# Layer 1: the output's affine step and its gate moved behind the transpose, with channels on partitions

## The chip, the cores and the metric

The kernel runs on one NeuronCore of one Trainium2 chip. The metric is the device time of one execution in microseconds (us); the time of the kernel before is the median of three executions.

## The reference, cut to what matters

Two transformer-like layers are applied to x, [8, 256, 256] (8 sequences of 256 tokens, 256 channels). The change lies in the attention half of layer 1, in its last lines:

```python
xc = silu(conv(xn) + conv_b)                       # causal conv of 4 taps, per channel
i_gate = sigmoid(xc @ ig_w.T + ig_b)
gamma  = sigmoid(xc @ gamma_w.T + gamma_b)
mem[t] = gamma[t] * mem[t-1] + i_gate[t] * k[t] * v[t]   # scan over tokens
out = _ln(mem, mn_g, mn_b) * q
o = (out - mean) / sqrt(var + 1e-05)               # per head of 16 channels
o = o * gn_g + gn_b                                # per channel (256)
o = o * sigmoid(xc @ og_w.T + og_b)                # output gate
return o @ Wo.T
```

The feed-forward half of layer 1 (704 hidden units, ternary weights) runs beside it on the same normalised input.

## The kernel before

Layer 0 comes first and fills the first two thirds of the program; the change does not touch it. A short preparation block then loads and splits the weights of layer 1 (a float32 matrix is carried as a high and a low part, `..._hi` and `..._lo`, and a product is three products of parts). Layer 1 follows in one block. The 2048 tokens are cut in GROUPS = 4 groups of 512 tokens (GT), each two sequences (`b` = 0, 1) or four tiles of 128 tokens (`t` = 0 to 3).

The groups are run as a software pipeline. `turns` calls `turn(late, early)` with (None, 0), then three times in a hardware loop with (i, i + 1), then with (3, None). The early part of a turn does projections, convolution, norms, gates and the feed-forward of a group; the late part does the scan, the two norms behind it, the output product and the store of the group before. So there are five turns: the first with an early part alone, three loop turns with both, and the last with a late part alone. In this text they are turn 0, loop turns 1, 2 and 3, and the last turn.

Each engine has its own instruction stream, written out by hand in one order per turn, and works it in that order. Between engines there are only semaphores: `wait(name, k)` holds the engine until `name` has been raised k times in this turn; `inc` raises it. A held instruction holds all behind it on its engine.

PSUM has eight banks, `lbank` in the profile. The four tiles' gate products take banks 2 and 3 in turn (`gate(t)`): 128 tokens on partitions, 256 columns of input gate and 256 of output gate, with both biases added by one more matmul (`ones_rows` by `bias`, L1673). The scalar engine's sigmoid (L1333) writes both halves to `gates`. `gated(engine, late, b)` (L1196 to L1203) is the affine step and the gate, three tensor-by-tensor operations on [128, 512] in SBUF, recorded in the profile at L1151; the gain and the shift lie in `par`, copied to all partitions. GpSimd does it for b = 0 and the vector engine for b = 1. `o_turn(b)` (L1697) then transposes `o` by TensorE into bank 4 + b, `output_high` (scalar engine, L1348) and `output_low` (vector engine, L1528) split it, and `output(b)` multiplies by Wo (L1591), `residual(b)` (L1536) adds x, and SyncE stores.

Names that the prediction uses, on each engine in program order, at the end of a loop turn: on the vector engine `output_normed` (its last operation is L1523), `hidden(4)` (L1469), `gated(1)`, `hidden(5)`, `values(1)` (four operations at L1151: two on `rows` with `par`, two on `qk`), `output_low(0)` and `(1)`, `residual`, `mlp_added`. On TensorE `gate(0)`, `gate(1)`, `ffn_up(5)` (L1641, which waits for `hidden(4)`), `gamma(1)`, `o_turn(0)`, `o_turn(1)`, `gate(2)`, `gate(3)`, `output(0)`, `output(1)`, `ffn_down` (L1655). On the scalar engine `sigmoid(5)` (L1290), `gate(0)`, `gate(1)`, `output_high(0)`, `hidden_high(5)` (L1297), `output_high(1)`, `decays(1)` (L1314), `gate(2)`, `gate(3)`. On GpSimd `gated(0)`, `hidden_low(4)`, `hidden_low(5)` (L1167), `through_input_gate(0)` and `(1)` (L1184).

Of the kernel before, what the change touches and what calls it, by code (L numbers as in the profile page):

```python
# [15 lines left out]
P = 128  # L16
D = 256
# [41 lines left out]
G16, G256 = 4 * L1_DH, 2 * D  # L59
N_LOADS = 6  # L60
# [871 lines left out]
def layer1(nc, dram, keep, out):  # L932

    X, ident = keep["X"], keep["ident"]
    with ExitStack() as ctx:
        def sb(name, shape, dt=F32):
# [12 lines left out]
        bias = sb("bias", [P, 2 * D], F32R)  # L949
        conv = sb("conv", [P, KC, TAPS + 1])  # L950
        gamma_b = sb("gamma_b", [P, KC])
        par = sb("par", [P, G16 + G256])
        vn_g, vn_b, mn_g, mn_b = (par[:, L1_DH * n:L1_DH * n + L1_DH].rearrange("p (a d) -> p a d", a=1)
                                  .to_broadcast([P, PAIR_HEADS, L1_DH]) for n in range(4))
        gn_g, gn_b = par[:, G16:G16 + D], par[:, G16 + D:G16 + 2 * D]
        gn_g2, gn_b2 = (x.rearrange("p (a d) -> p a d", a=1).to_broadcast([P, BPG, D]) for x in (gn_g, gn_b))
# [16 lines left out]
                   vn_done=BPG, gamma_done=KC, decay_done=KC, io_done=TPG, gates_done=TPG,  # L973
# [5 lines left out]
                   ro_done=1, on_done=BPG, o_link0=2, o_link1=2, o_done0=1, o_done1=1,  # L979
# [3 lines left out]
        with ExitStack() as prep:  # L983
# [7 lines left out]
            bias_raw = tmp("bias_raw", [P, 2 * D])  # L991
            bias_b = tmp("bias_b", [P, 2 * D], F32R)
# [4 lines left out]
            @block.sync  # L997
            def _(sp):
                sp.dma_start(shared[:], dram["l1w"].rearrange("p k n -> p (k n)")).then_inc(once["raw_loaded"], 16)
                sp.dma_start(rows3[:].bitcast(BF16)[:, 0:3 * UPC], dram["signs"]).then_inc(once["signs_loaded"], 16)  # L1000
                sp.wait_ge(once["zeroed"], 1)
                loads = [(const2[:], dram["const2"]), (wo_raw[:], dram["wo"]),
                         (conv[:], dram["conv"]), (gamma_b[:], dram["gamma_b"])]
                loads.append((par[:], dram["scales_shifts"].partition_broadcast(P)))
                loads.append((bias_raw[0:2, :], dram["gate_bias"]))
                assert len(loads) == N_LOADS
                for dst, src in loads:
                    sp.dma_start(dst, src).then_inc(once["loaded"], 16)
                prime(sp, list(S.values()))

            @block.gpsimd
            def _(pool):
                pool.memset(bias_raw[:], 0.0).then_inc(once["zeroed"], 1)
                pool.memset(half[:], -0.5).then_inc(once["zeroed"], 1)
                pool.memset(eps16[:, 0:2 * PAIR_HEADS], 0.0).then_inc(once["zeroed"], 1)
# [11 lines left out]
                pool.tensor_scalar(gn_g, gn_g, 4.0, None, ALU.mult)  # L1027
                pool.wait_ge(once["w_hi_done"], 2)
                pool.tensor_tensor(wo_lo[:], wo_raw[:], wo_hi[:].bitcast(F32), ALU.subtract).then_inc(once["w_lo_done"], 1)
# [49 lines left out]
        gates = sb("gates", [P, 2, TPG, D])  # L1079
# [100 lines left out]
        def through_input_gate(engine, early, b):  # L1180
            wait = waiter(engine, early)
            wait("gates_done", 2 * b + 2)
            wait(f"kv_done{b}", 1)
            inc(engine.tensor_tensor(vn[:, pair(b), :], qk[:, 1, pair(b), :], gates[:, 0, pair(b), :], ALU.mult), f"b_done{b}")  # L1184
# [30 lines left out]
        @block.gpsimd  # L1215
        def _(pool):
            pool.memset(xpad[:, :, :, 0:PAD], 0.0).then_inc(pad_zeroed, 1)

            def turn(late, early):
                def convolved():  # L1220
                    wait = waiter(pool, early)
                    for k in range(KC):
                        wait("conv_sig", k + 1)
                        inc(pool.tensor_tensor(cs[:, k, :], cv[:, k, :], cs[:, k, :], ALU.mult), "xc_done")
                    for k in range(KC):
                        wait("xc_hi_done", k + 1)
# [12 lines left out]
                if late is not None:  # L1239
                    gated(pool, late, 0)  # L1240
                if early is not None:
                    hidden_low(pool, early, 4)
                    hidden_low(pool, early, 5)
                    through_input_gate(pool, early, 0)
                    through_input_gate(pool, early, 1)

            turns(pool, turn)

        @block.scalar
        def _(act):  # L1250
            act.wait_ge(pad_zeroed, 1)

            def turn(late, early):
# [45 lines left out]
                def convolved():  # L1299
# [4 lines left out]
                    wait("io_done", 0)  # L1304
# [20 lines left out]
                def gate(t):  # L1325
                    wait = waiter(act, early)
                    wait("io_done", t + 1)
                    if t == 0:
                        wait("o_done0", 0)
                        wait("o_done1", 0)  # L1330
                        wait("b_done0", 0)
                        wait("b_done1", 0)
                    inc(act.activation(gates[:, :, t, :], turned(banks[2 + t % 2][:]), ACT.Sigmoid), "gates_done")  # L1333
# [39 lines left out]
                if early is not None:  # L1373
# [5 lines left out]
                    gate(0)  # L1379
                    gate(1)  # L1380
                if late is not None:
                    output_high(0)
                if early is not None:
                    hidden_high(5)
                if late is not None:
                    output_high(1)
                if early is not None:
                    decays(1)
                    gate(2)
                    gate(3)  # L1390
# [4 lines left out]
        def _(dve):  # L1395
            def turn(late, early):
# [171 lines left out]
                if late is not None:  # L1568
                    gated(dve, late, 1)
                if early is not None:  # L1570
                    hidden(5)
                    values(dve, early, 1)
# [12 lines left out]
        def _(pe):  # L1585
# [15 lines left out]
            def turn(late, early):  # L1601
# [9 lines left out]
                def query_key(t):  # L1611
# [5 lines left out]
                    else:  # L1617
                        wait("gates_done", 0)
# [45 lines left out]
                def gate(t):  # L1664
                    wait = waiter(pe, early)
                    if t < 2:
                        wait("qk_sq", TPG)
                        wait("xc_lo_done", KC)
                    else:
                        wait("gates_done", t - 1)  # L1670
                    bank = banks[2 + t % 2][:]
                    product(bank, rows(xc_hi, xc_lo, t), cols(W_IO, W_G), last=False)
                    inc(pe.matmul(bank, ones_rows[:], bias[:], start=False, stop=True), "io_done")  # L1673
# [43 lines left out]
                if early is not None:  # L1717
# [12 lines left out]
                    gate(0)  # L1730
                    gate(1)
# [5 lines left out]
                if early is not None:  # L1737
                    gate(2)
                    gate(3)
# [24 lines left out]
def layouts(inputs, np):  # L1764
# [44 lines left out]
    a["scales_shifts"] = np.concatenate([l1["attn_" + n] for n in ("vn_g", "vn_b", "mn_g", "mn_b", "gn_g", "gn_b")]).reshape(1, -1)  # L1809
    a["gate_bias"] = np.repeat(np.concatenate([l1["attn_ig_b"], l1["attn_og_b"]]).reshape(1, -1), 2, axis=0)  # L1810
# [30 lines left out]
```

## Time and profile before

| what | value |
|---|---|
| median of 3 executions | 938.91 us (937.0 to 942.07) |
| profiled execution, its own time | 938.2 us |
| its span, first to last instruction | 936.4 us |
| mean granted clock of TensorE | 0.917 of full |
| busy: PE (TensorE) | 763.0 us |
| busy: DVE (vector engine) | 699.5 us |
| busy: ACT (scalar engine) | 452.4 us |
| busy: POOL (GpSimd) | 419.0 us |

Busy time is a sum over the whole program. Layer 1 begins with its preparation at about 611 us and its five turns run from about 629 us to the end; what one of its turns costs is read from the order of the work in that turn, not from these sums. The 1.8 us between span and time lie around the instructions.

### The profile page before, as it was taken

How to read it: one execution, taken by the hardware profiler on the slowest of the kernel's cores; microseconds unless marked ns; L12 is line 12 of the kernel's file. 1: busy time of each engine (PE TensorE's matmuls, PEld its weight loads, DVE VectorE, ACT ScalarE, POOL GpSimd, SP SyncE). 2: the span in 40 equal slices, each digit the busy share in tenths (PEclk: the TensorE clock that was granted, in tenths of full speed). 3: DMA queues.
4: the chain of work that ended last, by engine and by line, in shares of the span. 5: the costliest groups of instructions: out<-in, count | busy, mean ns of one | idle time of the engine just before them, and what ended most of it. 6: DMA issues, size and time to landing. Idle time of an engine off the chain costs nothing. (4 is left out here: it accounts for less than half of the span.)

```text
span 936.4 us, 15623 instructions
## 1 busy us (share of the span) xinstructions
PE 763.0 (81%) x5602; PEld 653.7 (70%) x5602; DVE 699.5 (75%) x1146; ACT 452.4 (48%) x717; POOL 419.0 (45%) x335
## 2 busy tenths in 40 slices
PE   3278989999999999999999999918683883893842
PEld 3166878888888888888888888806572672682642
DVE  6988866876776766776776766346689889879866
ACT  4256546556657556557556565535342342332301
POOL 2244533443466756662542543342616616606622
PEclk9999989999999999999999999958796896796775
DMA  4111210110110110110000000030000000000000
GB/s 150 34 35 36 86 42 25 53 42 2 30 36 19 47 42 19 47 30 3 20 18 12 11 19 3 1 147 1 1 1 0 8 15 0 0 22 0 0 22 23
DMA packets 21383, 25.82 MB, mean 28 GB/s; under 512 B 4418, under 2 KB 17090, under 8 KB 21060
## 3 DMA queue, kind: packets, MB, share of 16 engines
q1 hardware_dynamic: 21316, 24.93, 9.0%
q8 instruction: 41, 0.67, 0.3%
q14 instruction: 26, 0.21, 0.1%
HBM read 14.83 MB, written 3.28 MB: 19 GB/s over the span
## 5 line engine op out<-in xcount | busy, mean ns | idle before, releaser
L593 DVE TENSOR_REDUCE neg_max<-s_pair 128x4 f32<-128x1024 f32 x127 | 155.0, 1220 | 81.4 <-PE s_pair L805 81.1
L446 ACT ACTIVATE probs<-t_pair 128x1024 f32<-128x1024 f32 x128 | 131.3, 1026 | 139.8 <-PE t_pair L830 139.6
L345 POOL TENSOR_TENSOR hid<-g,hid 128x512 f32<-128x512 f32 x64 | 82.3, 1286 | 185.5 <-DVE g L704 143.9
L339 POOL TENSOR_TENSOR hid_lo<-hid,hid_hi 128x512 fp32r<-128x512 f32 x64 | 85.9, 1342 | 96.1 <-ACT hid_hi L456 96.0
L805 PE MATMUL s_pair<-K,Q 96*128 96x256 f32 x508 | 85.5, 292 | 14.0 <-DVE neg_max L593 9.4
L805 PEld LDWEIGHTS s_pair<-K,Q 96*128 96x128 f32 x508 | 76.6, 196 | 22.8 <-issue 7.3
L830 PE MATMUL t_pair<-Q,K 104*128 104x512 f32 x256 | 86.5, 420 | 0.3 <-DMA Q<-max_parts 0.3
L872 PE MATMUL down<-w_hi,hid_hi 128*128 128x256 f32 x256 | 83.9, 328 | 0.7 <-POOL hid_lo L339 0.7
L872 PE MATMUL down<-w_lo,hid_hi 128*128 128x256 f32 x256 | 72.1, 282 | 0.0
L872 PE MATMUL down<-w_hi,hid_lo 128*128 128x256 f32 x256 | 72.1, 282 | 0.0
L1151 POOL TENSOR_TENSOR rows<-rows,par 128x512 f32<-128x512 f32 x24 | 36.2, 1509 | 79.5 <-DVE rows L1499 52.4
L845 PE MATMUL misc<-probs,V 128*32 128x256 f32 x1024 | 69.1, 388 | 0.8 <-DVE xn_lo L543 0.5
L872 PEld LDWEIGHTS down<-w_hi,hid_hi 128*128 128x128 f32 x256 | 48.2, 188 | 26.4 <-issue 24.7
L1641 PE MATMUL lbank<-l_xn_hi,tern 128*128 128x512 f32 x96 | 38.0, 484 | 25.1 <-DVE l_hid L1469 25.1
L733 PE MATMUL gate<-xn_hi,w_hi 128*128 128x256 f32 x256 | 56.9, 304 | 0.0
L696 DVE SCALAR_TENSOR_TENSOR g<-g,gate 128x512 f32<-128x512 f32 x64 | 42.7, 668 | 18.6 <-ACT g L459 18.5
L467 ACT ACTIVATE g<-g 128x512 f32<-128x512 f32 x64 | 40.2, 628 | 26.6 <-DVE g L696 26.6
L733 PE MATMUL up<-xn_hi,w_hi 128*128 128x256 f32 x256 | 52.8, 289 | 0.0
L733 PE MATMUL up<-xn_lo,w_hi 128*128 128x256 f32 x256 | 52.3, 286 | 0.0
L733 PE MATMUL up<-xn_hi,w_lo 128*128 128x256 f32 x256 | 52.3, 287 | 0.0
L733 PE MATMUL gate<-xn_hi,w_lo 128*128 128x256 f32 x256 | 51.4, 282 | 0.0
L733 PE MATMUL gate<-xn_lo,w_hi 128*128 128x256 f32 x256 | 51.3, 282 | 0.0
(244 smaller groups left out, 2058.2 us busy)
## 6 DMA issues: line engine op xcount, KB each, us to landing
stage<-in_ternary SPq DMA_DIRECT2D x18, 256.0 KB, 2.9
Q<-q_hi SPq DMA_DIRECT2D x64, 64.0 KB, 2.0
stage<-in_scales SPq DMA_DIRECT2D x8, 384.0 KB, 3.4
X<-in_x SPq DMA_DIRECT2D x8, 256.0 KB, 3.7
Q<-q_lo SPq DMA_DIRECT2D x32, 64.0 KB, 2.0
Q<-max_parts SPq DMA_DIRECT2D x128, 4.0 KB
out<-res SPq DMA_DIRECT2D x8, 256.0 KB, 2.2
shared<-in_l1w SPq DMA_DIRECT2D x1, 1536.0 KB, 6.2
```

The lines of the kernel that those rows point to most:

```text
L339: pool.tensor_tensor(hid_lo[:, m % 2, :, :].rearrange("p a n -> p (a n)"), hid[:, m % 2, :], hid_hi[:, m % 2, :, :].rearrange("p a n -> p ...
L345: pool.tensor_tensor(hid[:, m % 2, :], g[:, m % 2, :], hid[:, m % 2, :], ALU.mult).then_inc(S["hid_done"], 1)
L446: act.activation(probs[:, u % 2, th, :], t_pair[:], ACT.Exp, scale=SCALE).then_inc(S["probs_done"], 1)
L467: act.activation(g[:, m % 2, :], g[:, m % 2, :], ACT.Tanh, scale=GELU_B).then_inc(S["t_done"], 1)
L593: dve.tensor_reduce(neg_max[:, u % 2, 4 * jp:4 * jp + 4], score_banks(u, jp)[:].rearrange("p (s n) -> p s n", n=SEQ), AX_X, ALU.max, negat ...
L696: dve.scalar_tensor_tensor(out=g[:, m % 2, :], in0=g[:, m % 2, :], scalar=1.0, in1=gate[:], op0=ALU.add, op1=ALU.mult).then_inc(S["u_done" ...
L733: mm = pe.matmul(out, lhs[a][k], rhs[b][k], start=(n == 0), stop=(n == 3 * KC - 1))
L805: mm = pe.matmul(score_banks(u, jp)[:, 512 * j + SEQ * s:512 * j + SEQ * s + SEQ], Q[0:KROWS, quad, 2 * jp + j, P * s:P * s + P], K[0:KROW ...
L830: mm = pe.matmul(t_pair[:, 512 * jp:512 * jp + 512].rearrange("p (j n) -> p j n", j=2), K[rows, quad, hq, P * th:P * th + P], Q[rows, quad ...
L845: mm = pe.matmul(misc[32 * j:32 * j + 32, 0:SEQ], V[:, th, h, :], probs[:, u % 2, th, SEQ * j:SEQ * j + SEQ], start=(th == 0), stop=(th == ...
L872: mm = pe.matmul(down[:, D * t:D * t + D], h[:, m % 2, n, P * t:P * t + P], w[:, a, n, 2 * D:3 * D], start=(a == 0 and t == 0 and n == 0 a ...
L1641: mm = pe.matmul(banks[bank][:], w[:, k, P * c:P * c + P], x[:, k, :], start=(n == 0), stop=(n == 3))
```

## The change

The affine step and the gate are done after the transpose, where a channel is a partition. The gain, the shift and the output gate's bias then are one number per partition (`out_cols`, a new small load). The steps are now:

- `o_turn(b)` waits for the normed output alone.
- `output_affine(b)`, scalar engine, new: two operations on [128, 256] from PSUM, with scale and bias from `out_cols`, to `oa` in SBUF.
- `output_gated(b)`, vector engine, new: one product of `oa` and `out_gate` on [128, 512], for both b. GpSimd has no part in it any more.
- `output_high` and `output_low` read `oa` instead of the PSUM bank.
- The gate products: `input_gate(b)` makes the input gate of two tiles in one bank (28 matmuls of 256 columns for all four, with the bias matmul as before); `output_gate(m)` makes the output gate of 128 channels by 512 tokens (6 matmuls of 512 columns each), with its bias in the scalar engine's sigmoid.

```diff
-        def gated(engine, late, b):
-            wait = waiter(engine, late)
-            wait("on_done", b + 1)
-            y = o[:, pair(b), :]
-            inc(linked(engine, wait, f"o_link{b}", [
-                (y, y, gn_g2, ALU.mult),
-                (y, y, gn_b2, ALU.add),
-                (y, y, gates[:, 1, pair(b), :], ALU.mult)]), f"o_done{b}")
...
-                if late is not None:
-                    gated(pool, late, 0)
...
+                def output_gate(m):
+                    wait = waiter(act, early)
+                    wait("og_done", m + 1)
+                    if m == 0:
+                        wait("o_done", 0)
+                    inc(act.activation(out_gate[:, m, :], banks[2 + m][:], ACT.Sigmoid, bias=out_cols[:, m, 2:3]), "out_gate")
...
+                def output_affine(b):
+                    wait = waiter(act, late)
+                    wait("o_turned", b + 1)
+                    for m in range(KC):
+                        inc(act.activation(oa[:, b, m, :], banks[4 + b][:, SEQ * m:SEQ * m + SEQ], ACT.Identity,
+                                           scale=out_cols[:, m, 0:1], bias=out_cols[:, m, 1:2]), "oa_done")
+
                 def output_high(b):
                     wait = waiter(act, late)
-                    wait("o_turned", b + 1)
-                    inc(act.activation(o_hi[:, b, :, :], turned(banks[4 + b][:]), ACT.Copy), "o_hi_done")
+                    wait("o_done", b + 1)
+                    inc(act.activation(o_hi[:, b, :, :], oa[:, b, :, :], ACT.Copy), "o_hi_done")
...
+                def output_gated(b):
+                    wait = waiter(dve, late)
+                    wait("oa_done", 2 * b + 2)
+                    wait("out_gate", KC)
+                    inc(dve.tensor_tensor(oa[:, b, :, :], oa[:, b, :, :], out_gate[:, :, SEQ * b:SEQ * b + SEQ], ALU.mult), "o_done")
...
-                    inc(dve.tensor_tensor(o_lo[:, b, :, :], turned(banks[4 + b][:]), o_hi[:, b, :, :].bitcast(F32), ALU.subtract), "o_lo_done")
+                    inc(dve.tensor_tensor(o_lo[:, b, :, :], oa[:, b, :, :], o_hi[:, b, :, :].bitcast(F32), ALU.subtract), "o_lo_done")
...
+                def input_gate(b):
+                    wait = waiter(pe, early)
+                    wait("qk_sq", TPG)
+                    wait("xc_lo_done", KC)
+                    for t in range(2 * b, 2 * b + 2):
+                        dst = banks[2 + b][:, D * (t % 2):D * (t % 2) + D]
+                        product(dst, rows(xc_hi, xc_lo, t), cols(W_IO, W_IO + D), last=False)
+                        mm = pe.matmul(dst, ones_rows[:], bias[:], start=False, stop=True)
+                    inc(mm, "in_done")
+
+                def output_gate(m):
+                    wait = waiter(pe, early)
+                    wait("in_gate", m + 1)
+                    at = W_IO + D + P * m
+                    inc(product(banks[2 + m][:], cols(at, at + P), [lambda k, x=x: x[:, k, :] for x in (xc_hi, xc_lo)]), "og_done")
...
                 def o_turn(b):
                     wait = waiter(pe, late)
-                    wait(f"o_done{b}", 1)
+                    wait("on_done", b + 1)
```

The vector engine's instructions at the end of the loop's body, before the change (`rows` is `o` or `vn`; the value in brackets is the semaphore that an instruction waits for; REGISTER_ALU rows compute a semaphore's value):

```order
L1469 TENSOR_TENSOR l_hid<-sig,lbank 128x512 [waits l_h_lo_done2,l_sig_done]
L1151 TENSOR_TENSOR rows<-rows,par 128x512 [waits l_on_done]
L1151 TENSOR_TENSOR rows<-rows,par 128x512 [waits l_o_link1]
L1151 TENSOR_TENSOR rows<-rows,gates 128x512 [waits l_o_link1]
L1131 REGISTER_ALU
L1469 TENSOR_TENSOR l_hid<-sig,lbank 128x512 [waits l_h_lo_done3,l_sig_done]
L1151 TENSOR_TENSOR rows<-rows,par 128x512 [waits l_qk_copied,l_vn_done]
```

The same place after the change:

```order
L1474 TENSOR_TENSOR l_hid<-sig,lbank 128x512 [waits l_h_lo_done2,l_sig_done]
L1132 ISA
L1534 TENSOR_TENSOR oa<-oa,out_gate 128x512 [waits l_out_gate,l_oa_done]
L1132 REGISTER_ALU
L1474 TENSOR_TENSOR l_hid<-sig,lbank 128x512 [waits l_h_lo_done3,l_sig_done]
L1132 REGISTER_ALU
L1534 TENSOR_TENSOR oa<-oa,out_gate 128x512 [waits l_out_gate,l_oa_done]
L1152 TENSOR_TENSOR rows<-rows,par 128x512 [waits l_qk_copied,l_vn_done]
```

The three operations of `gated(1)` are gone; a gate product now stands on either side of the second `l_hid`, and both wait for `oa_done`, which the scalar engine raises.

The scalar engine at the same place, before the change:

```order
L1290 ACTIVATE sig<-lbank 128x512 [waits l_up_done]
L1333 ACTIVATE gates<-lbank 128x2x256 [waits l_b_done0,l_o_done1,l_b_done1,l_o_done0,l_io_done]
L1333 ACTIVATE gates<-lbank 128x2x256 [waits l_io_done]
L1348 ACTIVATE o_hi<-lbank 128x512 [waits l_o_turned]
L1297 ACTIVATE h_hi<-l_hid 128x512 [waits l_hid_done]
L1348 ACTIVATE o_hi<-lbank 128x512 [waits l_o_turned]
L1314 ACTIVATE shared<-lbank,gamma_b 128x512 [waits l_gamma_done]
```

And after it (`oa` is what `output_affine` writes):

```order
L1280 ACTIVATE sig<-lbank 128x512 [waits l_up_done]
L1322 ACTIVATE gates<-lbank 128x512 [waits l_b_done1,l_b_done0,l_in_done]
L1322 ACTIVATE gates<-lbank 128x512 [waits l_in_done]
L1345 ACTIVATE oa<-lbank,out_cols 128x256 [waits l_o_turned]
L1345 ACTIVATE oa<-lbank,out_cols 128x256
L1287 ACTIVATE h_hi<-l_hid 128x512 [waits l_hid_done]
L1345 ACTIVATE oa<-lbank,out_cols 128x256 [waits l_o_turned]
L1345 ACTIVATE oa<-lbank,out_cols 128x256
L1351 ACTIVATE o_hi<-oa 128x512 [waits l_o_done] x2
```

The affine operations of b = 0 took the place of `output_high(0)`; those of b = 1 stand behind `hidden_high(5)` (`h_hi`), and both high parts stand behind them.

TensorE around `o_turn`, in the loop's body, before the change:

```order
L1641 MATMUL lbank<-l_xn_lo,tern 128x512 x2
L1591 MATMUL lbank<-xc_hi,l_hi 128x512 [waits l_vn_done,l_xc_lo_done]
...
L1697 MATMUL lbank<-ident,rows 128x128 [waits l_o_done0]
L1697 MATMUL lbank<-ident,rows 128x128 x3
L1697 MATMUL lbank<-ident,rows 128x128 [waits l_o_done1]
L1697 MATMUL lbank<-ident,rows 128x128 x3
L1591 MATMUL lbank<-l_hi,xc_hi 128x512 [waits l_gates_done]
```

And after it:

```order
L1655 MATMUL lbank<-l_xn_lo,tern 128x512 x2
L1605 MATMUL lbank<-xc_hi,l_hi 128x512 [waits l_vn_done,l_xc_lo_done]
...
L1716 MATMUL lbank<-ident,rows 128x128 [waits l_on_done]
L1716 MATMUL lbank<-ident,rows 128x128 x3
L1716 MATMUL lbank<-ident,rows 128x128 [waits l_on_done]
L1716 MATMUL lbank<-ident,rows 128x128 x3
L1605 MATMUL lbank<-xc_hi,l_hi 128x512 [waits l_in_gate]
```

The transposes kept their place behind `ffn_up(5)` (`tern`) and `gamma(1)` (`xc_hi,l_hi`); only what they wait for became an earlier step, and the gate product behind them is the output gate's.

## Rows read from the trace of the kernel before

**Rows 1.** Page, part 1: busy us, share of span, instructions.

```profile
PE 763.0 (81%) x5602; PEld 653.7 (70%) x5602; DVE 699.5 (75%) x1146; ACT 452.4 (48%) x717; POOL 419.0 (45%) x335
```

**Rows 2.** Chain of waits, loop turns 1, 2, 3: start us, us, what.

```profile
733.22 0.60 DVE l_hid L1469
...
744.83 3.11 PE lbank L1591 x24
...
803.75 0.60 DVE l_hid L1469
...
808.75 0.68 DVE l_hid L1469
...
810.55 0.70 DVE rows L1151
811.28 1.73 DVE qk L1151
813.03 1.68 DVE qk L1151
814.71 0.61 DVE o_lo L1528
815.37 4.63 PE lbank L1591 x24
...
875.77 0.60 DVE l_hid L1469
...
887.39 4.71 PE lbank L1591 x24
```

**Rows 3.** Timeline, loop turn 2, all engines: start, us, engine, line, what.

```profile
803.23 3.35 POOL L1151 TENSOR_TENSOR rows<-rows,par 128x512 f32<-128x512 f32 x2 [3.68 <-DVE rows L1523]
804.41 0.73 PE L1641 MATMUL lbank<-l_xn_hi,tern 128*128 128x512 f32 x2 [2.05 <-DVE l_hid L1469]
...
809.32 1.03 PE L1697 MATMUL lbank<-ident,rows 128*128 128x128 f32 x8
...
809.96 0.61 ACT L1348 ACTIVATE o_hi<-lbank 128x512 fp32r<-128x512 f32 x1
...
811.15 1.30 POOL L1167 TENSOR_TENSOR h_lo<-l_hid,h_hi 128x512 fp32r<-128x512 f32 x1 [1.18 <-ACT h_hi L1297]
...
812.40 1.76 POOL L1184 TENSOR_TENSOR rows<-qk,gates 128x512 f32<-128x512 f32 x1
...
813.21 0.39 PE L1673 MATMUL lbank<-bias,ones_rows 128*128 128x512 f32 x1
```

**Rows 4.** Groups by form, ACT: count, then busy us, mean ns, idle before.

```profile
L477 ACT ACTIVATE o_sb<-misc 128x256 f32<-128x256 f32 x64 | 24.5, 383 | 18.4 <-PE misc L845 17.6
...
L1333 ACT ACTIVATE gates<-lbank 128x512 f32<-128x512 f32 x16 | 9.2, 600 | 7.2 <-PE lbank L1673 4.5 <-DVE rows L1151 2.7
...
L1314 ACT ACTIVATE shared<-lbank,gamma_b 128x512 f32<-128x512 f32 x8 | 5.6, 694 | 10.6 <-PE lbank L1591 10.6
```

**Rows 5.** Windows, PE: stretch, us, busy us (count), granted clock, DMA, GB/s.

```profile
792.80:798.50 5.70, 5.69 (x14) 0.50 0.00 0
...
744.83:747.70 2.87, 2.87 (x24) 1.00 0.02 6
887.39:891.90 4.51, 4.51 (x24) 0.62 0.00 0
927.75:932.60 4.85, 4.85 (x24) 0.55 0.02 7
```

**Rows 6.** Timeline, the last turn.

```profile
920.19 3.31 POOL L1151 TENSOR_TENSOR rows<-rows,par 128x512 f32<-128x512 f32 x2 [7.63 <-DVE rows L1523]
...
925.23 1.97 PE L1697 MATMUL lbank<-ident,rows 128*128 128x128 f32 x8 [23.20 <-POOL rows L1151]
926.38 0.60 ACT L1348 ACTIVATE o_hi<-lbank 128x512 fp32r<-128x512 f32 x1 [11.29 <-PE lbank L1697]
927.01 0.69 DVE L1528 TENSOR_TENSOR o_lo<-lbank,o_hi 128x512 fp32r<-128x512 f32 x1 [1.29 <-ACT o_hi L1348]
```

More of the change, by code:

```diff
@@ L948, in layer1 @@
         wo_lo = sb("wo_lo", [P, KC, D], F32R)
-        bias = sb("bias", [P, 2 * D], F32R)
+        bias = sb("bias", [P, D], F32R)
         conv = sb("conv", [P, KC, TAPS + 1])
         gamma_b = sb("gamma_b", [P, KC])
-        par = sb("par", [P, G16 + G256])
+        par = sb("par", [P, G16])
+        out_cols = sb("out_cols", [P, KC, 3])
         vn_g, vn_b, mn_g, mn_b = (par[:, L1_DH * n:L1_DH * n + L1_DH].rearrange("p (a d) -> p a d", a=1)
                                   .to_broadcast([P, PAIR_HEADS, L1_DH]) for n in range(4))
-        gn_g, gn_b = par[:, G16:G16 + D], par[:, G16 + D:G16 + 2 * D]
-        gn_g2, gn_b2 = (x.rearrange("p (a d) -> p a d", a=1).to_broadcast([P, BPG, D]) for x in (gn_g, gn_b))
         tern = sb("tern", [P, 3 * UPC], F32R)
@@ L1026, in _ @@
                     pool.tensor_scalar(scale, scale, 4.0, None, ALU.mult)
[L1027 removed]
+                pool.tensor_scalar(out_cols[:, :, 0], out_cols[:, :, 0], 4.0, None, ALU.mult)
                 pool.wait_ge(once["w_hi_done"], 2)
@@ L1078, in layer1 @@
         vn, o = (x.rearrange("p (a d) -> p a d", d=D) for x in (vn, o))
-        gates = sb("gates", [P, 2, TPG, D])
+        gates = sb("gates", [P, TPG, D])
+        out_gate = sb("out_gate", [P, KC, GT])
+        oa = sb("oa", [P, BPG, KC, SEQ])
         mem = mem_rows.rearrange("p (k n) -> p k n", k=KC)
@@ L1181, in through_input_gate @@
             wait = waiter(engine, early)
-            wait("gates_done", 2 * b + 2)
+            wait("in_gate", b + 1)
             wait(f"kv_done{b}", 1)
-            inc(engine.tensor_tensor(vn[:, pair(b), :], qk[:, 1, pair(b), :], gates[:, 0, pair(b), :], ALU.mult), f"b_done{b}")
+            inc(engine.tensor_tensor(vn[:, pair(b), :], qk[:, 1, pair(b), :], gates[:, pair(b), :], ALU.mult), f"b_done{b}")
         def memory_scaled(engine, late, b):
@@ L1303, in convolved @@
                         inc(act.activation(cs[:, k, :], cv[:, k, :], ACT.Sigmoid), "conv_sig")
-                    wait("io_done", 0)
+                    wait("in_done", 0)
+                    wait("og_done", 0)
                     for k in range(KC):
@@ L1323, in queries_kept @@
                     inc(act.activation(rq[:], ss[:, :, 0:PAIR_HEADS], ACT.Copy), "q_kept")
-                def gate(t):
+                def input_gate(b):
                     wait = waiter(act, early)
[L1327 to L1330, printed above, removed]
+                    wait("in_done", b + 1)
+                    if b == 0:
                         wait("b_done0", 0)
                         wait("b_done1", 0)
-                    inc(act.activation(gates[:, :, t, :], turned(banks[2 + t % 2][:]), ACT.Sigmoid), "gates_done")
+                    inc(act.activation(gates[:, pair(b), :], turned(banks[2 + b][:]), ACT.Sigmoid), "in_gate")
+                def output_gate(m):
[4 more added lines that the diff above has]
+                    inc(act.activation(out_gate[:, m, :], banks[2 + m][:], ACT.Sigmoid, bias=out_cols[:, m, 2:3]), "out_gate")
                 def memory_squared(b):
@@ L1378, in turn @@
                     hidden(5)
-                    gate(0)
-                    gate(1)
+                    input_gate(0)
+                    input_gate(1)
                 if late is not None:
-                    output_high(0)
+                    output_affine(0)
                 if early is not None:
@@ L1385, in turn @@
                 if late is not None:
+                    output_affine(1)
+                    output_high(0)
                     output_high(1)
@@ L1388, in turn @@
                     decays(1)
-                    gate(2)
-                    gate(3)
+                    output_gate(0)
+                    output_gate(1)
             turns(act, turn)
@@ L1568, in turn @@
                 if late is not None:
-                    gated(dve, late, 1)
+                    output_gated(0)
                 if early is not None:
                     hidden(5)
+                if late is not None:
+                    output_gated(1)
+                if early is not None:
                     values(dve, early, 1)
@@ L1617, in query_key @@
                     else:
-                        wait("gates_done", 0)
+                        wait("out_gate", 0)
                     inc(product(banks[2 + t % 2][:], rows(xn_hi, xn_lo, t), cols(W_QK, W_V)), "qk_done")
@@ L1662, in gamma, with input_gate @@
                     inc(product(banks[m][:], cols(W_G + P * m, W_G + P * m + P), [lambda k, x=x: x[:, k, :] for x in (xc_hi, xc_lo)]), "gamma_done")
-                def gate(t):
+                def input_gate(b):
                     wait = waiter(pe, early)
[L1666 to L1673, printed above, removed]
+                    wait("qk_sq", TPG)
[10 more added lines that the diff above has]
+                    inc(product(banks[2 + m][:], cols(at, at + P), [lambda k, x=x: x[:, k, :] for x in (xc_hi, xc_lo)]), "og_done")
                 def b_turn(b):
@@ L1729, in turn @@
                     ffn_up(4)
-                    gate(0)
-                    gate(1)
+                    input_gate(0)
+                    input_gate(1)
                     ffn_up(5)
@@ L1737, in turn @@
                 if early is not None:
-                    gate(2)
-                    gate(3)
+                    output_gate(0)
+                    output_gate(1)
                 if late is not None:
```

19 lines of the change are left out of this document (10 added, 9 removed).

## The prediction

> **What bounds the kernel now.** First the page's busy times: TensorE is busy for 763 us and the vector engine for 700 [rows 1], but these are sums over two layers, and the change touches layer 1 alone. There the view to read is the chain of waits [rows 2]: the reader is to see that from `l_hid` at 803.75 to `o_lo` at 814.71 every step is the vector engine's, without a gap that matters, and that TensorE then takes the chain over with the 24 matmuls of the output product at 815.37. The stretch recurs in each loop turn: from the start of `hidden(4)` to the start of the output product it is 744.83 - 733.22 = 11.61 us, 815.37 - 803.75 = 11.62 and 887.39 - 875.77 = 11.62 [rows 2]. Behind it stand, in a line, output product, `ffn_down`, residuals, normalisation and transposes of the next turn; nothing there starts early when this stretch is late. So a microsecond here is a microsecond of the turn, three times. I call the start of `hidden(4)` T; in loop turn 2 T is 803.75.
>
> Then the timeline of the same stretch [rows 3], for where the transposes come. TensorE starts `ffn_up(5)` at 804.41, when `hidden(4)` has ended, works through it and `gamma(1)`, and starts the eight transposes at 809.32, T+5.57. They weren't waiting for `gated`: GpSimd's three operations ended near 808.3 (two from 803.23 in 3.35 us, then one more of half that) and the vector engine's before `hidden(5)` at 808.75, and TensorE was busy with `gamma(1)` until the transposes. So removing the affine step in front of them moves them by next to nothing. That is the row on which the forecast rests.
>
> **What is removed.** The vector engine loses `gated(1)`: from 803.75 + 0.60 to 808.75, 4.4 us in each loop turn [rows 2]. GpSimd loses the same three operations (3.35 us for the first two [rows 3]), beside them.
>
> **What is added, in a loop turn.** I follow the new order by hand, with durations from the rows.
> 1. TensorE: the input gates are 28 matmuls of 256 columns in place of 14 of 512, the same columns. `ffn_up(5)` still waits for `hidden(4)`. Transposes at T+5.57. In the old timeline `output_high(0)` starts at 809.96 [rows 3], which I take as the landing of b = 0's four transposes: T+6.2.
> 2. Scalar engine, `output_affine(0)`: two operations of 256 columns from PSUM with two per-partition operands. No row has this form. A plain copy of that size takes 0.383 us, and one per-partition operand (the bias of `decays`) lifts 0.600 to 0.694 [rows 4], so 0.383 + 2 x 0.094 = 0.57 us each; neighbours overlap by about 0.1 (`o_hi` and its successors start closer than they last). The pair: 1.05 us, ending at T+7.3. Bounds: 0.77 with the operands free, 1.2 at two full operations of 0.60.
> 3. Vector engine: it finishes `hidden(4)` at T+0.6 and the next instruction is `output_gated(0)`, which waits for that pair. It stands still from T+0.6 to T+7.3, 6.7 us, with `hidden(5)` and all of `values(1)` queued behind the wait. The 4.4 us that it saved lie inside this gap. Then one product of two SBUF tiles, 0.70 us alone (as the free one at 810.55 [rows 2]): T+8.0.
> 4. `hidden(5)`, 0.6: T+8.6. Only now can the scalar engine do `hidden_high(5)` (0.63) and, queued behind it, `output_affine(1)` (1.05): T+10.2. The vector engine waits again, 1.6 us.
> 5. `output_gated(1)` then meets GpSimd, which got `h_hi(5)` late as well and runs `hidden_low(5)` (1.30 [rows 3]) to about T+10.6. Next to a GpSimd operation a two-SBUF product of the vector engine lasts until that one ends and some 0.55 more (1.68 us in place of 0.70 [rows 2]). So it ends at T+11.1. The first operation of `values(1)` waits in the same way for `through_input_gate(0)` (1.76 [rows 3]): T+12.8. The other three now run beside an idle GpSimd, 0.70 each, where `qk` took 1.73 and 1.68 [rows 2]: T+14.9. Here the change gives 2 us back.
> 6. `output_low(0)` ends 0.7 later and TensorE starts at T+15.55. `output_low(1)` now reads two SBUF tiles and can be held by `through_input_gate(1)`, to about T+17.2, but `output(1)` isn't due before T+18. The high parts lie under `values(1)`.
>
> So the stretch grows from 11.62 to 15.55: **+3.9 us in each loop turn, 11.8 in three**. With no contention at all it would be 10.2 + 0.7 + 4 x 0.7 + 0.7 = 14.4 (+2.8); with `values(1)` as contended as before (5.3 us, from the end of `hidden(5)` at 808.75 + 0.68 to 814.71) it is 11.1 + 5.3 + 0.7 = 17.1 (+5.5). I take the middle case because GpSimd has just one operation left to run beside `values(1)`.
>
> A rule bears on steps 5 and 6. The Trainium skill, GPSIMD Engine Reference, Specifications, states that GpSimd's SBUF interfaces are shared with VectorE and contend with vector instructions that have two SBUF inputs. The change turns `output_low` from one PSUM and one SBUF input into such an instruction. By that rule `output_low(1)` pays up to another microsecond; by the old row it would cost 0.61. The output product doesn't wait for it, so the sum is the same either way.
>
> **TensorE's clock.** Today the output product follows 1.8 us of idleness (the last gate matmul issues at 813.21) and its 24 matmuls take 3.11, 4.63 and 4.71 us in the chain [rows 2], at a granted clock of 1.00 in the first loop turn and 0.62 in the third [rows 5]. In the new order TensorE's last work before it is the output gates, 12 matmuls from about T+6.4 to T+9.2, so it idles for 6.3 us. Where it had idled long it restarts at the lower level: 0.50 over the 5.7 us from 792.80, and 0.55 over the output product of the last turn, 4.85 us long [rows 5]. I price the product at 5.0 in each loop turn: 15.0 - 12.45 = **+2.6**. Bounds: 0 if the clock falls no more than now, +4.1 if it stays low 0.5 us into `ffn_down` too.
>
> **The last turn** has nothing in TensorE's queue. The transposes start when the normed output is there, 920.2 where `gated(0)` started [rows 6]. Four of them and the hand-over took 1.15 (926.38 - 925.23 [rows 6]): 921.35. Affine pair: 922.4; the second pair and the first high part behind it on the scalar engine: 923.9; `output_gated(1)` ended by 924.1; `output_low(0)` 0.69 [rows 6]: 924.8. Output product at 924.85, not one `o_lo` after 927.01, 927.75: **-2.9**.
>
> **The rest.** The output gates need no bias matmul, two of 0.23 us between starts (the one at 813.21 is the last of its kind in a turn [rows 3]); where the chain runs through TensorE alone, in turn 0, that is -0.5. The bias vector in the preparation is half as long, -0.2; the extra load of `out_cols` ends beside the weight split. Together **-0.7**. The sigmoid of the output gate gets a bias operand, +0.09 each, at the end of the scalar engine's turn, hidden behind `values(1)`.
>
> **Sum**: 11.8 + 2.6 - 2.9 - 0.7 = +10.8. On the profiled execution's own 938.2 (span 936.4) that is 949.0; this execution lies 0.7 under the median of the runs, so I say 949.5.
>
> **The rivals.**
> - Fewer operations are faster. Nothing stalls, the vector engine trades 4.4 us for two products of 0.7: -3.0 per loop turn, so 938.9 - 9.0 - 2.9 - 0.7 = 926. The Trainium skill, VectorE: DVE Perf Modes, Rules for kernel authors, says "Minimize op *count*, not sems", which points this way. It decides if the transposes land by T+0.6; the rows put them at T+6.2. 5 in 100.
> - The stall is there, but contention goes and the clock stays: 8.4 - 3.6 = +4.8, 943.7. 15 in 100.
> - The stall lies beside other work, so that time stays near 938. It would need TensorE to do `ffn_down` first, and its order puts the output product in front. 4 in 100.
> - All of `values(1)` stays contended and the clock costs most: 16.5 + 4.1 - 3.6 = +17, 956. 8 in 100.
> - My forecast, 945 to 954: 68 in 100.
>
> **Numbers.** 0.5% (4.7 us) is about what a measurement of this kernel tells from no change. The range 942.5 to 955 leaves out the fast rival, the hidden stall and most of the last. Faster: 0.05. Same: the hidden stall and part of the second rival, 0.10. Slower: 0.85.
>
> **What would show it.** In the changed profile: the vector engine idle for 6 to 7 us before the first `oa<-oa,out_gate`, released by the scalar engine's `oa`; 1 to 2 us before the second; the transposes still about 5.6 us after `hidden(4)`; `qk` operations of the vector engine at 0.7 us; 15 to 16 us from `hidden(4)` to the output product; that product at about 0.5 of the clock. It is wrong if the transposes start within 2 us of T, or if the output product starts before T+13.

## The result and the profile after

The changed kernel takes 950.0 us (median of 4 runs, 947.83 to 952.89) against 937.95 us before (4 runs, 934.45 to 942.07). The ratio is 1.0141, 95% interval 1.011 to 1.0172: slower by 1.4%, 12 to 13 us. The profiled execution took 951.88 us, with a span of 950.1; it is 1.9 us above the median.

The page's first part, of the changed kernel (busy us, share of span, instructions; it answers to [rows 1]):

```profile
PE 761.9 (80%) x5650; PEld 656.7 (69%) x5650; DVE 687.3 (72%) x1142; ACT 460.6 (48%) x733; POOL 398.2 (42%) x323
```

The vector engine has 12 us less to do than before, GpSimd 21 us less, TensorE no more; the scalar engine has 8 us more. The sum over all four went down and the time went up. That is what the busy times can't show and the chain can. The chain of waits of the changed kernel, the stretch from `hidden(4)` to the output product in loop turn 2 (start us, us, what):

```profile
812.02 0.61 DVE l_hid L1474
812.68 3.46 PE lbank L1655 x8
816.14 1.61 PE lbank L1605 x6
817.75 0.45 PE lbank L1716 x4
818.23 1.03 ACT oa L1345 x2
819.89 0.69 DVE l_hid L1474
820.60 0.63 ACT h_hi L1287
821.24 0.92 ACT oa L1345 x2
...
823.05 1.76 DVE rows L1152
824.84 0.70 DVE rows L1152
825.56 0.70 DVE qk L1152
826.29 0.69 DVE qk L1152
826.98 0.61 DVE o_lo L1539
827.64 5.49 PE lbank L1605 x24
```

Before, this stretch was one engine's [rows 2]. Now it goes through three: TensorE's `ffn_up(5)` and `gamma(1)`, the transposes, the scalar engine's affine pair, back to the vector engine, to the scalar engine for `h_hi` and the second pair, and back again. It lasts 827.64 - 812.02 = 15.62 us, where it was 11.62.

The timeline of the same place shows who stands still (the bracket at a row's end is the idle time before it, and its releaser):

```profile
817.59 1.03 PE L1716 MATMUL lbank<-ident,rows 128*128 128x128 f32 x8
818.23 1.02 ACT L1345 ACTIVATE oa<-lbank,out_cols 128x256 f32<-128x256 f32 x2 [0.47 <-PE lbank L1716]
819.28 0.69 DVE L1534 TENSOR_TENSOR oa<-oa,out_gate 128x512 f32<-128x512 f32 x1 [6.66 <-ACT oa L1345]
...
821.31 1.27 POOL L1168 TENSOR_TENSOR h_lo<-l_hid,h_hi 128x512 fp32r<-128x512 f32 x1 [6.67 <-ACT h_hi L1287]
822.04 0.62 ACT L1351 ACTIVATE o_hi<-oa 128x512 fp32r<-128x512 f32 x1
822.18 0.95 DVE L1534 TENSOR_TENSOR oa<-oa,out_gate 128x512 f32<-128x512 f32 x1 [1.61 <-ACT oa L1345]
822.54 1.72 POOL L1185 TENSOR_TENSOR rows<-qk,gates 128x512 f32<-128x512 f32 x1
...
826.90 2.37 DVE L1539 TENSOR_TENSOR o_lo<-oa,o_hi 128x512 fp32r<-128x512 f32 x2
827.13 1.59 POOL L1185 TENSOR_TENSOR rows<-qk,gates 128x512 f32<-128x512 f32 x1 [2.87 <-DVE qk L1152]
827.64 0.80 PE L1605 MATMUL lbank<-wo_hi,o_hi 128*128 128x256 f32 x2 [6.26 <-DVE o_lo L1539]
```

The vector engine stands still 6.66 us ahead of the first gate product and 1.61 ahead of the second, both until `oa`; in loop turns 1 and 3 it is 7.75 and 5.10 us ahead of the first. The transposes start 5.57 us after `hidden(4)`, the same as before [rows 3], although nothing but their place in TensorE's queue holds them now. And TensorE idles 6.26 us ahead of the output product. Its clock in the three output products of the loop and in the last turn's (windows: stretch, us, busy and count, granted clock, DMA, GB/s; they answer to [rows 5]):

```profile
751.64:756.20 4.56, 4.56 (x26) 0.63 0.00 0
827.64:833.10 5.46, 5.46 (x25) 0.50 0.08 29
903.21:908.70 5.49, 5.49 (x26) 0.50 0.09 32
941.27:946.50 5.23, 5.23 (x24) 0.53 0.09 32
```

### The profile page after: what moved, and what is told of

Same layout as the page of the kernel before. It is cut to its first block and busy times, and to the rows that moved or that the text cites. A ratio compares the mean times of both kernels' runs of the same rounds, so it can differ in the third digit from the quotient of the medians.

```text
span 950.1 us, 15728 instructions
## 1 busy us (share of the span) xinstructions
PE 761.9 (80%) x5650; PEld 656.7 (69%) x5650; DVE 687.3 (72%) x1142; ACT 460.6 (48%) x733; POOL 398.2 (42%) x323
## 5 line engine op out<-in xcount | busy, mean ns | idle before, releaser
L1168 POOL TENSOR_TENSOR h_lo<-l_hid,h_hi 128x512 fp32r<-128x512 f32 x20 | 27.6, 1382 | 56.0 <-ACT h_hi L1287 56.0
```

## The experiments

Two theories. Mine: the time is lost by order. An instruction that waits for a late result stands in front of work that could have run, on engines that each keep one order, and the idling that follows lowers TensorE's clock. The rival: the new operations themselves, and their contention with GpSimd, cost the time wherever they stand. Nine kernels tell these apart. Each ratio is to the kernel before, run on the same chip beside it.

| run | median us | ratio to before | 95% interval |
|---|---|---|---|
| the change | 950.0 | 1.0141 | 1.011 to 1.0172 |
| dve_values_first | 938.57 | 1.0015 | 0.9999 to 1.0031 |
| pe_hoist | 945.86 | 1.0088 | 1.006 to 1.0116 |
| pe_act_hoist | 933.16 | 0.9937 | 0.9916 to 0.9958 |
| all_hoist | 918.71 | 0.9799 | 0.9772 to 0.9825 |
| warm | 949.57 | 1.0142 | 1.0109 to 1.0175 |
| warm_filled | 945.35 | 1.0078 | 1.0054 to 1.0102 |
| pool_through_first | 945.49 | 1.0092 | 1.0061 to 1.0122 |
| affine_twice | 955.62 | 1.02 | 1.0169 to 1.023 |
| before_values_last | 928.51 | 0.9909 | 0.988 to 0.9939 |

### dve_values_first: the vector engine's work ahead of its wait

```diff
                     hidden(4)
-                if late is not None:
-                    output_gated(0)
-                if early is not None:
                     hidden(5)
-                if late is not None:
-                    output_gated(1)
-                if early is not None:
                     values(dve, early, 1)
                 if late is not None:
+                    output_gated(0)
+                    output_gated(1)
                     output_low(0)
```

> The changed kernel with one edit in the vector engine's order: both output_gated stand behind hidden(5) and values(1), so that it works while it would wait for the affine step. Theory (the cost is the order: what is queued behind the wait): the output product starts near T+12.2 in place of T+15.5 (T is the start of hidden(4)), 3.3 us less in each loop turn and about 1 us of clock in all, so 939 us. Rival (the new operations and their contention cost the time, wherever they stand): no change, 950.

938.6 us: the same instructions, 1.2% less time. The vector engine's timeline in loop turn 2 of this run:

```profile
812.18 0.69 DVE L1474 TENSOR_TENSOR l_hid<-sig,lbank 128x512 f32<-128x512 f32 x1 [3.44 <-ACT sig L1280]
812.78 1.41 DVE L1152 TENSOR_TENSOR rows<-rows,par 128x512 f32<-128x512 f32 x2
...
815.56 0.69 DVE L1534 TENSOR_TENSOR oa<-oa,out_gate 128x512 f32<-128x512 f32 x1
...
816.81 1.14 DVE L1534 TENSOR_TENSOR oa<-oa,out_gate 128x512 f32<-128x512 f32 x1 [0.57 <-ACT oa L1345]
```

The 6.66 us of idling have become 3.44 ahead of `hidden(5)` and none ahead of the first gate product. The output product starts 12.6, 11.5 and 11.7 us after `hidden(4)` in the three loop turns, where the theory had 12.2 and the change has 16.7, 15.6 and 14.1. The rival falls: the operations and their engines are unchanged, and contention is still on the path (in loop turn 2 `output_gated(1)` takes 1.14 us and `output_low(0)` 1.68). This version cannot be told from the kernel before, ratio 1.0015.

### pe_hoist, pe_act_hoist, all_hoist: the late step itself moved up

`pe_hoist`, TensorE's order:

```diff
                     input_gate(1)
+                if late is not None:
+                    o_turn(0)
+                    o_turn(1)
+                if early is not None:
                     ffn_up(5)
                     gamma(1)
-                if late is not None:
-                    o_turn(0)
-                    o_turn(1)
```

> The changed kernel with one edit in TensorE's order: both o_turn stand ahead of ffn_up(5) and gamma(1). If TensorE's order alone makes the affine step late, the stall of 6.7 us falls to about 1 and the time to 933. My theory: the scalar engine's own order (sigmoid(5), which waits for ffn_up(5), and two input gates stand ahead of the affine step) holds it too, so the stall shortens by 0.9 us a turn only: 947.

`pe_act_hoist`, also the scalar engine's:

```diff
                     queries_kept()
+                if late is not None:
+                    output_affine(0)
+                    output_affine(1)
+                if early is not None:
                     hidden(5)
                     input_gate(0)
                     input_gate(1)
-                if late is not None:
-                    output_affine(0)
-                if early is not None:
                     hidden_high(5)
```

> pe_hoist, and on the scalar engine both output_affine ahead of hidden(5), that is before sigmoid(5) and the input gates. Theory: the affine step is done by T+2.4, no stall before the first gate product; hidden(5) then waits for its sigmoid and values(1) comes after it beside GpSimd, so the output product starts near T+12.4: 939. If the wait for the affine step weren't what costs the time: 950.

`all_hoist`, also both `output_high` ahead of `sigmoid(5)`, and the vector engine's:

```diff
                     hidden(4)
                 if late is not None:
                     output_gated(0)
-                if early is not None:
-                    hidden(5)
-                if late is not None:
                     output_gated(1)
+                    output_low(0)
+                    output_low(1)
                 if early is not None:
+                    hidden(5)
                     values(dve, early, 1)
-                if late is not None:
-                    output_low(0)
-                    output_low(1)
```

> pe_act_hoist, with both output_high ahead of sigmoid(5) on the scalar engine, and on the vector engine both output_gated and output_low ahead of hidden(5), values(1) last. Theory: the split output is ready near T+5, TensorE goes from the output gates to the output product without idling, near T+9.2 and at the full clock (about 3.0 us in place of 5.2): 6.2 + 2.2 us less in each loop turn, 925. That is 13 below the kernel before. If the vector engine's total work bounded the turn, it would stay near 938.

945.9, 933.2 and 918.7 us. TensorE's order moved alone gives little, since the scalar engine still holds the affine step behind `sigmoid(5)` and the input gates; in the timeline of `pe_hoist` the transposes start at 808.59, the pair only at 813.41, and the vector engine idles 4.74 us. Even that gain is only in part the earlier transposes: the output product starts 13.7 us after `hidden(4)` there, with `ffn_up(5)` and `gamma(1)` at the full clock, and in the change it starts 14.05 us after it in loop turn 3, at the same clock. With both moved (`pe_act_hoist`) the gate product, at 804.14, waits only 0.60. The full reordering, loop turn 2, timeline:

```profile
798.71 1.67 PE L1715 MATMUL lbank<-ident,rows 128*128 128x128 f32 x8 [1.67 <-DVE rows L1529]
...
799.40 2.03 ACT L1345 ACTIVATE oa<-lbank,out_cols 128x256 f32<-128x256 f32 x4 [0.16 <-PE lbank L1715]
...
800.45 0.69 DVE L1535 TENSOR_TENSOR oa<-oa,out_gate 128x512 f32<-128x512 f32 x1 [0.60 <-ACT oa L1345]
...
802.50 1.96 DVE L1540 TENSOR_TENSOR o_lo<-oa,o_hi 128x512 fp32r<-128x512 f32 x2 [0.34 <-ACT o_hi L1351]
...
807.46 0.40 PE L1604 MATMUL lbank<-wo_hi,o_hi 128*128 128x256 f32 x2
```

The reader is to see that the last row has no bracket: the output product follows the output gates without idling, 8.2 us after `hidden(4)` (9.2 expected), and the window from 807.46 shows 2.74 us at a clock of 1.00. This version beats the kernel before by 2.0% (0.9772 to 0.9825).

Two of the three came out 6 us lower than I had written. In `pe_act_hoist` the output product starts at 813.04, 10.1 us after `hidden(4)` in place of the 12.4 that I expected, and its `sigmoid(5)` starts at T+2.8 (805.75 - 802.94), where the kernel before had T+3.3: `ffn_up(5)` and `gamma(1)` ran at the full clock there, 3.3 us for what took 4.9 in [rows 3]. The transposes now stand in the 2 us gap ahead of them. That they keep the clock up by it is argued from these rows, not tested alone; and this profiled execution, at 929.24 us, lies 3.9 below the median of its runs, so its rows show more than the median gained.

### warm and warm_filled: TensorE's idling ahead of the output product

```diff
                     at = W_IO + D + P * m
+                    for _ in range(2 if late is not None else 0):
+                        product(banks[2 + m][:], cols(at, at + P), [lambda k, x=x: x[:, k, :] for x in (xc_hi, xc_lo)])
                     inc(product(banks[2 + m][:], cols(at, at + P), [lambda k, x=x: x[:, k, :] for x in (xc_hi, xc_lo)]), "og_done")
```

(`warm` has one extra set, `warm_filled` two. The last set counts, so the result is the same.)

> The changed kernel with each output gate's six matmuls done twice in the loop turns (the first set is overwritten by the second), so TensorE has 2.8 us more work in the 6.3 us before the output product and idles for 3.5. Theory (idling before the product lowers its clock): the product gets faster, between nothing and 2.2 us a turn, 944 to 948, although work is added. Rival (the lower clock has nothing to do with that gap): 950 and the same clock in the product.

> As the run with doubled output gates, but each output gate's six matmuls three times in the loop turns (the last set counts), so that TensorE is busy up to about 0.6 us before the output product. That run left the product at half clock after 3.3 us of idling. Theory (idling just ahead of the product is what lowers its clock): with the gap filled the product runs at the full clock, 3.0 us in place of 5.2 on average, 2.2 less in each loop turn: 943.5. Rival (something else sets the clock there): 950, product at half clock. If the added matmuls themselves were on the path, it would be above 950.

`warm` moved nothing, 949.6 us. Its output products, windows:

```profile
748.19:753.50 5.31, 5.31 (x25) 5.31 (x26) 2.32 (x2) 0.00 (x0) 1.08 (x1) 0.50 0.05 18
823.89:829.20 5.31, 5.31 (x25) 5.31 (x26) 2.33 (x2) 0.00 (x0) 1.08 (x1) 0.50 0.06 20
900.86:905.30 4.44, 4.44 (x25) 4.44 (x25) 2.32 (x2) 0.00 (x0) 1.08 (x1) 0.62 0.00 0
```

Each product follows 3.55 to 3.58 us of idling and stands at 0.50, 0.50 and 0.62 (the last number but two of a row), where the change, after 6.26, had 0.63, 0.50 and 0.50. That run alone would have spoken against the theory. With the gap filled:

```profile
750.93:754.00 3.07, 3.02 (x24) 2.83 (x24) 2.33 (x2) 0.00 (x0) 1.09 (x1) 1.00 0.00 0
824.40:827.50 3.10, 3.05 (x26) 2.86 (x25) 2.12 (x2) 0.00 (x0) 0.89 (x1) 1.00 0.00 0
```

The clock is 1.00. From its first matmul to `ffn_down` the product takes 3.3 us in each loop turn, in place of 4.6 to 5.5, after 0.82 to 0.85 us of idling. The added matmuls did not delay it: the three stretches from `hidden(4)` to the product add up to 46.55 us, in the change to 46.38. The kernel has 72 matmuls more and takes 945.4 us, ratio 1.0078 where the change's is 1.0141. So the lower clock in the output product costs the changed kernel 0.6%, about 6 us. Not all of that is new: the kernel before doesn't get the full clock there in every turn either [rows 5]. The product now also catches up with the vector engine: ahead of `output(1)` it waits for `output_low(1)`, about 0.2 us.

### pool_through_first: what contention costs

```diff
                     hidden_low(pool, early, 4)
-                    hidden_low(pool, early, 5)
                     through_input_gate(pool, early, 0)
+                    hidden_low(pool, early, 5)
                     through_input_gate(pool, early, 1)
```

> The changed kernel with through_input_gate(0) ahead of hidden_low(5) on GpSimd, so that it runs while the vector engine stands still. Theory (a two-SBUF operation waits for a GpSimd operation beside it): the first operation of values(1) takes 0.7 in place of 1.8 us, 1.1 us less a turn, 946.5. Without such contention: 950.

945.5 us. Its timeline in loop turn 2:

```profile
819.55 0.95 DVE L1534 TENSOR_TENSOR oa<-oa,out_gate 128x512 f32<-128x512 f32 x1 [1.60 <-ACT oa L1345]
820.42 1.40 DVE L1152 TENSOR_TENSOR rows<-rows,par 128x512 f32<-128x512 f32 x2
...
821.86 0.69 DVE L1152 TENSOR_TENSOR qk<-qk,ss 128x512 f32<-128x512 f32 x1
```

The two operations take 1.40 us, where in the change they took 1.76 + 0.70. That is 1.1 us a turn, 3.3 in the kernel; the measured 4.5 has the right sign and about the size. The three output products also had a higher clock, 0.63, 0.63 and 0.59 in place of 0.63, 0.50 and 0.50, 13.9 us in all against 15.6, so 1.7 less in this execution; why is not shown. So the 3.3 is the price of this meeting, and the rest of the 4.5 isn't.

### affine_twice: the scalar engine's operations

```diff
                     for m in range(KC):
+                        act.activation(osq[:, b, SEQ * m:SEQ * m + SEQ], banks[4 + b][:, SEQ * m:SEQ * m + SEQ], ACT.Identity,
+                                       scale=out_cols[:, m, 0:1], bias=out_cols[:, m, 1:2])
                         inc(act.activation(oa[:, b, m, :], banks[4 + b][:, SEQ * m:SEQ * m + SEQ], ACT.Identity,
```

> The changed kernel with every affine operation done twice on the scalar engine (the extra copy goes to a scratch tile that is free there). Theory (both affine pairs lie on the path): about 1.0 us more for each pair, 2 a loop turn and 2 in the last turn, so 958. If other work hid them: 950.

955.6 us, ratio 1.02: 5.6 us above the change, not 8. Both pairs lie on the path, but what the second pair added did not all arrive. From the transposes (816.41) the first gate product starts 2.61 us later, where it was 1.69, and the second 6.41, where it was 4.59; the output product starts 11.1 us later, where it was 10.05. In the last turn it starts 6.29 us after the transposes, where it was 4.47. Three times 1.05 and these 1.8 are 5.0, near what was measured. The missing 0.8 us of a turn is contention again. This run's timeline:

```profile
822.27 1.26 POOL L1185 TENSOR_TENSOR rows<-qk,gates 128x512 f32<-128x512 f32 x1
822.82 1.26 DVE L1536 TENSOR_TENSOR oa<-oa,out_gate 128x512 f32<-128x512 f32 x1 [2.51 <-ACT oa L1347]
824.00 1.40 DVE L1152 TENSOR_TENSOR rows<-rows,par 128x512 f32<-128x512 f32 x2
```

The vector engine comes later and waits once, for `through_input_gate(0)`; in the change it waited for `hidden_low(5)` and then for `through_input_gate(0)`, and from the second gate product to the end of the first two operations of `values(1)` it took 3.4 us, here 2.6.

### before_values_last: is the change needed for the better order?

The kernel before, with one move:

```diff
                     hidden(5)
-                    values(dve, early, 1)
                 if late is not None:
                     output_low(0)
                     output_low(1)
+                if early is not None:
+                    values(dve, early, 1)
+                if late is not None:
                     residual(0)
```

> The kernel before with one edit in the vector engine's order: both output_low ahead of values(1). Tells whether a better order needs the change at all. Theory: the old output product starts when TensorE has done gate(2) and gate(3), near T+9.9 in place of T+11.6, 1.7 us less in each loop turn, and up to 1.7 us a turn of clock, since TensorE no longer idles ahead of it: 929 to 933. If the stretch were bound by something else: 938.

928.5 us, ratio 0.9909. The output product follows the gates without a gap, in 2.84 us, at T+10.8, T+9.9 and T+9.9 in the three loop turns. So a little under half of what `all_hoist` gains over the kernel before can be had without the change, by moving `values(1)` alone. The rest, 0.9799 against 0.9909, needs the new form, where the transposes wait for nothing but the norm, or an order of the old one that wasn't tried.

## Why the prediction was right, step by step

The forecast was 949.5 us, in the range 942.5 to 955; the time is 950.0. The mechanism was right: the vector engine stands still behind a wait, and the output product comes late and at the lower clock. That the number fits to 0.5 us is in part luck. Between the two profiled executions the cost is 951.88 - 938.2 = 13.7 us, where the forecast adds up to 10.8; the terms below give 11.5 + 3.1 - 2.9 + 1.8 = 13.5. The median of the changed kernel then lies 1.9 us below its profiled execution. By its steps, profiled execution against profiled execution:

- **The transposes don't move.** Predicted T+5.57, measured 5.57 in loop turn 2 (817.59 - 812.02), but 6.66 (741.59 - 734.93) in turn 1 and 4.01 (893.17 - 889.16) in turn 3. In the kernel before it was 5.6 in all three. Only their queue holds them: `pe_hoist` starts them at once.
- **The affine pair**, priced at 1.05 us from rows that lacked the form: 1.02 and 1.00 in the timeline.
- **The stall**: predicted 6.7 and 1.6 us, measured 6.66 and 1.61. The clock of `ffn_up(5)` moves the first; the stretch to the output product is 751.64 - 734.93 = 16.71 us in loop turn 1, 15.62 in turn 2 and 903.21 - 889.16 = 14.05 in turn 3. The windows of `ffn_up(5)` and `gamma(1)` give the reason:

```profile
735.58:741.70 6.12, 6.12 (x16) 0.52 0.00 0
812.68:817.70 5.02, 5.02 (x16) 0.66 0.00 0
889.81:893.30 3.49, 3.49 (x16) 1.00 0.00 0
```

In the kernel before, the same matmuls took 4.91 us at 0.65 in all three turns. I had taken that for all three of the new ones, and turn 2 alone is like it. The signs I had named, 6 to 7 us of idling and 15 to 16 to the output product, hold in turn 2 only. The sum is right all the same, 46.4 - 34.9 = +11.5 us against 11.8, because turn 1 was 1.1 us longer and turn 3 1.6 us shorter than turn 2; that they cancel is luck.
- **Contention**: the first operation of `values(1)` was put at 1.7 us and took 1.76, the three behind it at 0.70 and took 0.70, 0.70 and 0.69. `output_low(1)` pays: the pair takes 2.37 us where it took 1.27 to 1.28. As written, the output product does not wait for that.
- **TensorE's clock**: the output products take 4.59 + 5.49 + 5.49 = 15.57 us in the chain, not 15.0, so +3.1 against 2.6. `warm_filled` shows the price by removing it.
- **The last turn**: from the first scan to the end 38.0 us before (936.4 - 898.40) and 35.1 after (950.1 - 915.03): -2.9, as predicted.
- **The rest** was the weak term: -0.7 predicted, +1.8 found (the first scan of loop turn 1 starts at 685.17 before and at 686.97 after). Turn 0 starts 0.8 us later (629.97 against 629.18), and 0.3 of that stands at the end of layer 0 already, before any changed instruction. The gates without their bias matmuls save 0.4, near the 0.5 predicted. In turn 0 `ffn_up(4)` took 3.38 us in the chain where it had taken 1.90; the clock was 0.50 there, against 0.99. In the other runs, most of which have the same turn 0, the same scan starts between 684.5 and 688.1, so a term of this size is below what one execution can show.
- **The rivals.** The fast one, fewer operations, needed the transposes to land by T+0.6, and they did not. In `pe_hoist` they land there, and the affine pair still starts only at T+4.3 (813.41, `hidden(4)` at 809.1); with the orders of the scalar and the vector engine changed too, the kernel takes 918.7: fewer operations are faster once hardly any of them waits. The rule of the Trainium skill, VectorE: DVE Perf Modes, Rules for kernel authors, is to minimise the count of chained operations. Taken as that rival takes it, for the time of the kernel, it would have given 926 for the change as it stands; the measurement decides against that reading. The rival that left the clock alone (943.7) is refuted by the products, 15.6 us in place of 12.45; the hidden stall (938) by the product's start at T+15.6 in place of T+11.6; the one with all of `values(1)` contended, by its last three operations at 0.70.

## What to carry to other kernels

Take operations off the engine that bounds a stage only after asking what its next instruction in line waits for: here 12 us of vector work were saved and each turn's stretch grew by 3.8 us on average, because the wait was placed in front of work that did not need it, and the producer had kept an old place in two other queues. When a result moves to other engines, move its place in the order of every engine on its way; TensorE's order alone gave 0.5%, the vector engine's alone 1.2%, all three orders 3.4%. And try the reordering on the old kernel too, since part of the gain may need nothing else.

## What the runs showed of the hardware

Idling TensorE for 3.6 us ahead of the output product lowered its clock as much as idling 6.3 us did (0.50 in loop turn 1 of `warm`, against 0.63 for the same product in the change); nearly halving the gap bought nothing, and filling it to 0.8 us bought 6 us. In `pool_through_first` a gap of 5.2 us gave products of 4.6 to 4.7 us. So the length of the gap did not set how long the lower level lasted. It did not decide alone whether the clock was low, either: after 3.1 us of idling in `pe_act_hoist` two of three products ran at 1.00 (loop turns 1 and 3, 0.63 in turn 2), and after 1.7 to 1.8 us the kernel before had 1.00 once and 0.62 to 0.63 twice [rows 5]. What decides between them no run here shows. The same code, `ffn_up(5)` and `gamma(1)`, ran at 0.52, 0.66 and 1.00 of the clock in three turns of one execution.

A vector operation with two SBUF inputs that meets a GpSimd operation lasts until that one ends and about 0.55 us more (`hidden_low(5)` ends at 822.58 and the gate product at 823.13), and the next GpSimd operation then waits for it in turn (1.72 in place of 1.27 us). Its cost is therefore a count of meetings: delaying the vector engine by 1.8 us in `affine_twice` delayed the output product by 1.05.
